# Gated cross attention with experts on one core: the second weight pair lands in the context slot, bias folds are shared by three engines, context transposes follow the query products, and 24 transposes of the identity come first

## What is computed

```python
x = x + tanh(g_xattn) * xattn(layernorm(x), ctx)
x = x + tanh(g_ffn) * ffn(layernorm(x))          # router, one of 8 experts per row

def xattn(char, sub):
    scores = (char @ Wq_c.T + bq_c) @ (sub @ Wk_s.T + bk_s).T / sqrt(512)
    char2sub = softmax(scores) @ (sub @ Wv_s.T + bv_s)
    scores2 = (sub @ Wq_s.T + bq_s) @ (char @ Wk_c.T + bk_c).T / sqrt(512)
    sub2char = softmax(scores2) @ (char @ Wv_c.T + bv_c)
    gate = sigmoid(concat(char2sub, sub2char) @ Wg.T + bg)
    return gate * char2sub + (1 - gate) * sub2char
```

## Time and profile before

| | us |
|---|---|
| median of 3 runs (lowest, highest) | 1189.27 (1188.73, 1190.29) |
| profiled execution | 1190.17 |
| its span in the profile | 1188.4 |
| TensorE busy (share of the span) | 1156.3 (97%) |
| VectorE busy | 716.0 (60%) |
| ScalarE busy | 451.1 (38%) |
| GpSimd busy | 199.2 (17%) |
| mean granted clock of TensorE over the span | 0.995 |

### The profile page before, as it was taken

How to read it: one execution, slowest core, us unless ns; L and a number is a source line. 1 busy time by engine, 2 the same in 40 slices (tenths; PEclk the granted TensorE clock), 3 DMA queues, 4 the chain that set the end, 5 groups by cost and what they waited for, 6 DMA issues and landing times.

```text
span 1188.4 us, 18063 instructions
## 1 busy us (share of the span) xinstructions
PE 1156.3 (97%) x5913; PEld 941.1 (79%) x5913; DVE 716.0 (60%) x1509; ACT 451.1 (38%) x800; POOL 199.2 (17%) x330
## 2 busy tenths in 40 slices
PE   6799999999999999999999999999999999998998
PEld 4678888888888888888888888888888887776776
DVE  6765655565457545763566466646565657787565
ACT  4333423443244324431444134423442344543342
POOL 2000000021001100110011011201020101266664
PEclk9899999999999999999999999999999999999999
DMA  6051102010201111011201020012010312586684
GB/s 231 18 169 55 45 28 98 10 48 27 79 26 39 35 62 44 21 35 62 62 21 35 26 97 20 30 33 97 9 39 0 134 45 76 196 268 186 178 238 128
DMA packets 59443, 90.63 MB, mean 76 GB/s; under 512 B 20522, under 2 KB 21062, under 8 KB 59400
## 3 DMA queue, kind: packets, MB, share of 16 engines
q1 hardware_dynamic: 49232, 64.25, 17.9%
q0 software_dynamic: 7264, 19.20, 5.0%
q10 hardware_dynamic: 2904, 6.63, 1.6%
HBM read 62.77 MB, written 29.12 MB: 77 GB/s over the span
## 4 chain that ended last, share of the span: by engine, by line
PE 92%; DVE 3%; issue 2%; another core or an unknown queue 1%; ACT 1%; POOL 0%; DMA 0%; ACTq 0%; DVEq 0%; POOLq 0%
PE mm L161 58%; PE u L980 15%; PE u L161 8%; PE tr L934 8%; PE mm L1754 1%; PE tr L161 1%; PE tr L1034 1%; DVE arena L380 0%; ACT pairs_as_f L1614 0%; DVE arena L1197 0%; DVE slot_as_f L372 0%; DMA slot_as_f<-in_L_xattn_bg 0%; DVE slot_as_f L1730 0%; ACTq L253 0%
## 5 line engine op out<-in xcount | busy, mean ns | idle before, releaser
L161 PE MATMUL mm<-arena 128*128 128x512 f32 x1536 | 375.4, 395 | 1.8 <-DVE arena L393 1.5
L161 PEld LDWEIGHTS mm<-arena 128*128 128x128 f32 x1536 | 282.7, 188 | 60.9 <-issue 2.8
L980 PE MATMUL u<-arena 128*128 128x512 f32 x768 | 189.8, 397 | 0.0
L161 PE MATMUL mm<-arena,q_pair 128*128 128x512 f32 x768 | 187.4, 399 | 0.0
L161 PEld LDWEIGHTS mm<-arena,q_pair 128*128 128x128 f32 x768 | 141.8, 188 | 31.8
L980 PEld LDWEIGHTS u<-arena 128*128 128x128 f32 x768 | 140.0, 188 | 27.4
L1197 DVE TENSOR_TENSOR arena<-tr,arena 128x512 fp32r<-128x512 f32 x144 | 96.7, 685 | 39.5 <-ACT arena L1093 17.5
L1197 DVE TENSOR_TENSOR arena<-mm,arena 128x512 fp32r<-128x512 f32 x64 | 44.2, 691 | 93.1 <-ACT arena L1084 89.9
L1080 ACT ACTIVATE q_pair<-mm,c_col 128x512 fp32r<-128x512 f32 x64 | 44.0, 688 | 132.8 <-PE mm L161 124.9
L1198 DVE SCALAR_TENSOR_TENSOR q_pair<-mm,c_col,q_pair 128x512 fp32r<-128x512 f32 x64 | 48.0, 750 | 70.2 <-ACT q_pair L1080 68.6
L161 PE MATMUL mm<-c2s_pair,arena 128*128 128x512 f32 x360 | 89.3, 397 | 0.0
(11 more groups left out here) (209 smaller groups left out, 1552.3 us busy)
## 6 DMA issues: line engine op xcount, KB each, us to landing
in_tile<-in_ctx SPq DMA_DIRECT2D x31, 256.0 KB, 2.6
x_tile<-in_x SPq DMA_DIRECT2D x29, 256.0 KB, 2.7
x_rows<-x_tile SPq DMA_DIRECT2D x29, 256.0 KB
in_tile<-in_x SPq DMA_DIRECT2D x28, 256.0 KB, 2.7
x_rows_early<-x_tile SPq DMA_DIRECT2D x28, 256.0 KB, 2.3
probs<-in_L_ffn_expert_b SPq DMA_DIRECT2D x21, 256.0 KB
slot_as_f<-in_L_ffn_expert_w SPq DMA_DIRECT2D x4, 1024.0 KB, 5.3
slot_as_f<-in_L_ffn_expert_w ACTq DMA_DIRECT2D x3, 1024.0 KB, 8.1
```

Source lines behind the costliest of these rows:

```text
L161: last = pe.matmul(bank, lhsT(a, c), rhs(b, c), start=start and n == 0, stop=stop and n == C * len(PASSES) - 1)
L980: last = pe.matmul(u_bank[m][:], v_pair[:, i % 2, a, tile(m)], pt_pair[:, i % 2, p], start=i == 0 and n == 0, stop=i == T - 1 and n == 2)
```

## The change

1. The raw second weights land in the two halves of the context slot CT instead of WV_S and WV_C. Their low parts no longer overwrite them. The first eviction of a context tile now waits for all 16 differences (`nat_lo`) and for 12 scalings.
2. The fold is split. `ACC` keeps only Wk_s times bq_c on VectorE (one instruction per chunk, a chain of four). A new step `SC` does the other three sums: ScalarE scales a chunk by its bias column into one of three buffers (12 passes in all, of which three write `folded` directly) and GpSimd adds it (nine additions of 128x512). `FOLD` becomes three steps: `FOLD0` the column of direction 0 (eight matmul records), `FOLD1` its constant and row, `FOLD2` all of direction 1. The row goes to the bank `mm0` instead of `u2`.
3. `CT0` to `CT3` move from between the queries to between the `A` steps, behind `Q03`. On TensorE `Q00` now waits for each chunk of A on its own.
4. `B` moves behind `AC02`; `AC00` no longer waits for `b_ready`. `AC02` stands ahead of the first x transposes, `XN0` behind `W02` and `XN1` to `XN3` ahead of all evictions on ScalarE. `AE` steps are mixed with `XT2`, `XT3`.
5. `WARM0`: 24 transposes of the identity on TensorE into `mm0`, which nobody reads, as soon as the identity is written.

The loads, their sizes and their order on SP are unchanged, and so is all work from `S00` on.

```diff
 def opening_steps():
-    names = """B0 W00 XS0 W01 AC00 XN0 XS1 W02 XN1 AC01 XS2 W03 XN2 XS3 XT0 XN3 XT1 AC02 ACC00 XT2 XT3 AC03
-               AE00 AE01 AE02 AE03 ACC01 ACC02 ACC03"""
+    names = """WARM0 W00 AC00 W01 XS0 AC01 W02 XS1 XN0 W03 XN1 XS2 XS3 XN2 XN3 AC02 B0 XT0 XT1 ACC00 AC03
+               AE00 AE01 XT2 XT3 AE02 AE03 ACC01 ACC02 ACC03 W10 SC00 SC01"""
...
-           [k.slot_as_f32[WV_S][:, LO], k.slot_as_f32[WV_C][:, LO]]]
+           [k.slot_as_f32[CT][:, HI], k.slot_as_f32[CT][:, LO]]]
...
+            elif kind == "SC":
+                for n in range(d + 1):
+                    if i == 0 and n == 0 and d == 0:
+                        act.wait_ge(b_ready, 1)
+                    to = folded[d][n]
+                    if i > 0:
+                        to = scaled[added[0] % SCALED]
+                        if added[0] >= SCALED:
+                            act.wait_ge(folded_up, added[0] - SCALED + 1)
+                        added[0] += 1
+                    act.activation(to, raw[d][n][:, i], ACT.Copy, scale=column(d, n, i)).then_inc(scaled_up, 1)
...
+            if kind == "SC" and c > 0:
+                for i in range(d + 1):
+                    n = added[0]
+                    if d == 0:
+                        pool.wait_ge(scaled_up, c + 1)
+                    else:
+                        pool.wait_ge(scaled_up, C + 2 * c + i + 1)
+                    if c > 1:
+                        pool.wait_ge(folded_up, n - d)
+                    pool.tensor_tensor(folded[d][i], folded[d][i], scaled[n % SCALED], ALU.add).then_inc(folded_up, 1)
+                    added[0] += 1
...
     if first:
-        names = """Q00 CT0 FOLD0 ACC10 W10 Q01 ACC11 W11 Q02 ACC12 W12 Q03 ACC13 W13 CT1 CT2 WT0 SM0 A10 XD0 XD1 WT1 A11 XD2
-                   XD3 CT3 FOLD10 AE10 AE11 WT2 A12 CD0 AE12 WT3 A13 CD1 AE13"""
+        names = """Q00 FOLD0 SC02 SC03 SC10 Q01 W11 SC11 Q02 W12 W13 Q03 WT0 FOLD1 SC12 SC13 A10 XD0 XD1 CT0 WT1 SM0 A11
+                   XD2 XD3 CT1 CT2 FOLD2 AE10 AE11 CD0 A12 AE12 WT2 CT3 CD1 A13 AE13 WT3"""
...
+                    if first and kind == "CT" and rel == 0 and i == 0:
+                        act.wait_ge(weights.nat_lo, 4 * C)
+                        act.wait_ge(weights.scaled_up, 3 * C)
```

More of the change, by code:

```diff
@@ L228, in weights_part, with column @@
     SMALL = 16 * 5
+    def column(d, n, c):
+        return b_cols[:, C * (2 * d + n) + c:C * (2 * d + n) + c + 1]
     def sync(sp):
@@ L424, in run @@
             elif kind == "FOLD":
[L425 to L426 removed]
+                if i == 0:
+                    pe.wait_ge(folded_col, C)
                     pe.wait_ge(group_lo, C)
[L428 to L431 removed]
+                else:
+                    pe.wait_ge(folded_up, (C - 1, 3 * (C - 1))[i - 1])
+                    pe.wait_ge(fold_read, i)
+                at = i // 2
+                if i != 1:
+                    for m in range(C):
+                        last = pe.matmul(bank[3][:, m:m + 1], folded[at][1][:, m * P:(m + 1) * P], ones[:, 0:1],
+                                         start=True, stop=True)
+                if i != 0:
+                    pe.matmul(bank[3][:, C:C + 1], ones, b_const[:, at:at + 1], start=True, stop=True)
+                    last = pe.matmul(row_bank[:], ones, folded[at][0], start=True, stop=True)
+                last.then_inc(fold_mm, 1)
+            elif kind == "WARM":
+                pe.wait_ge(consts, 1)
+                for n in range(WARM):
+                    pe.transpose(b_bank[:, 0:P], ident[:], ident[:])
         return run
     part = Part(sync, scalar, vector, gpsimd, tensor)
+    part.nat_lo, part.scaled_up, part.fold_read = nat_lo, scaled_up, fold_read
     part.group_mm, part.group_lo, part.router_split = group_mm, group_lo, router_split
@@ L948, in run @@
                         pe.wait_ge(xt_lo, 4 * b + 4)
-                    if i == 0 and here == 0:
-                        pe.wait_ge(weights_group_lo, C * (d + 1))
                     product(pe, bank[:], lambda a, c: arena[:, A_X + d, a, c, tile(i)],
-                            lambda p, c: arena[:, queries_of(d), p, c]).then_inc(q_mm, 1)
+                            lambda p, c: arena[:, queries_of(d), p, c], before=lambda c: (
+                                pe.wait_ge(weights_group_lo, C * d + c + 1) if i == 0 and here == 0 else None
+                            )).then_inc(q_mm, 1)
                 elif kind == "V":
@@ L960, in run @@
                         pe.wait_ge(ct_lo, 4 * b + 4)
+                        if here == 0:
+                            pe.wait_ge(weights.fold_read, 3)
                     product(pe, bank[:], lambda a, c: q_pair[:, a, c, tile(i)],
```

81 lines of the change are left out of this document (37 added, 44 removed).

## The result

| | before | after |
|---|---|---|
| median of the four runs each (lowest, highest), us | 1189.78 (1188.73, 1191.56) | 1183.10 (1182.02, 1183.87) |
| profiled execution and its span, us | 1190.17, 1188.4 | 1182.02, 1180.3 |

The ratio is 0.9942, with a 95% interval of 0.9924 to 0.9959: 0.6% faster, a small difference that the interval sets apart from none. Two more comparisons, each on its own chip time with its own runs of the kernel before, gave 0.9924 (0.9906 to 0.9942) and 0.9946 (0.9932 to 0.9959). The forecast of 1182.3 lies 0.8 from the median, inside its own range of 1181.3 to 1183.8.

A forecast was written before the change was run, and what follows sets the result against it. TensorE was taken as the bound, with only its idle or slow time in the first 67 us to win. S0 at 60.2, 7.0 sooner, gives 1189.27 - 7.0 = 1182.3 us; own range 1181.3 to 1183.8, wide range 1178.9 to 1186.3.

The forecast's parts named there:

- VectorE's four chores per chunk: Ahead of 48.80: two fold multiply-adds and two differences per chunk of second weights make TensorE's 6.16 us hole; two remain.
- Start to Q00: Opening: Q00 needs all four x tiles and starts at 24.8, 2.0 us sooner; the earlier AC00 is worth nothing by itself.
- The cold stretch: Around Q00: TensorE, nearly idle from 19.0 to 24.8, drops its clock; Q00 and the work behind it charged 1.6 us.
- Rival (a): Gap ahead of Q00: the clock stays up or TensorE's opening fills the gap, giving back 1.6: 1180.7 us; chance 0.25.
- ScalarE ahead of A10: From 31.3: three evictions, six scaling passes at 0.80 and six copies take 10.3 us before the last difference; A10 at 42.4.
- x: Ahead of FOLD2: time of one GpSimd addition of 128x512, taken as 1.2 us between bounds of 0.48 and 1.7.
- collisions: GpSimd additions beside VectorE differences, at chunks 1 to 3 and the row sums: each costs 0 to 1.2, charged 1.1 in all.
- WT5's late load: Behind S0: a doubt that work there, such as a late load of WT5, loses what was won; no size given.
- (b): GpSimd is the new bound: x at 1.7 to 2.5 puts FOLD2 2.0 to 5.2 later, 1184.3 to 1187.5 us; chance 0.15.
- (c): Scaling passes cost a plain copy and nothing collides: 1.3 + 0.8 + 1.1 less, 1179.1 us; chance 0.11.
- (d): Slower than before: VectorE's instructions hold off the additions, needing x above 3.5 us; chance 0.04 together with (e).
- (e): The change does nothing since another wait is behind the hole ahead of 48.80; chance 0.04 together with (d).

The follow-up runs named there:

- b4_small_fold: Kernel before, with VectorE's six chained multiply-adds of the second direction done on 2 of 512 columns (sums left out); 1188.21 us, ratio 0.9966.
- b_first: Changed kernel with the bias transpose B0 back in first place of the opening, ahead of W00; 1186.09 us, ratio 0.9955.
- Small_adds: Changed kernel with GpSimd's nine fold additions done on 2 of 512 columns (most fold sums left out); 1182.37 us, ratio 0.9926.
- fill_gaps: Changed kernel with 32 more idle transposes in TensorE's gaps between AC03 and Q00; 1184.48 us, ratio 0.9948.
- early_xt: Changed kernel with evictions XT0 and XT1 ahead of normalisations XN2 and XN3 on ScalarE; 1181.60 us, ratio 0.9910.

## Why the prediction was right

By its own steps, in the profiled execution of the changed kernel:

| step | forecast | measured |
|---|---|---|
| AC00 | 6.65 | 6.82 |
| XN3 ends | 19.95 | 20.64 |
| Q00 | 24.8 | 25.36 |
| clock at 0.50 | 22 to 29 | 21.7 to 28.6 |
| Q01 | 30.4 to 30.9 | 30.69 |
| hole ahead of A10; A10 | 1.8; 42.4 | 1.00; 41.65 |
| FOLD2's wait for GpSimd; FOLD2 | under 1; 50.2 | 0.23; 49.89 |
| S0 | 60.2 | 60.31 |
| S0 to S1 | 3.23 | 3.89 |

The mechanism held: VectorE's four chores per chunk set the old hole (b4_small_fold), two of them left it, and A10 waits for the differences and not for the fold. The forecast also named the fall of the clock, the waits' releasers and the size of the whole. But several terms were mis-sized and made up for each other:

- **Start to Q00.** Forecast 2.0 sooner, measured 1.4. The loads of chunk 1 landed later (its copies start at 7.75, not 7.24), and with them all that follows: XN3 ended 0.7 late, and Q00 came 4.72 behind it, where the forecast had 4.85. And the place of B0 was not worth nothing but about 0.4 (b_first).
- **The cold stretch.** Charged with 1.6, worth 0 to 1.1. The error is in the step that has FOLD0 "ready to run, because VectorE's three chained multiply-adds end at 28.7": they end at 29.7, since GpSimd's first addition holds one of them off (3.31 for 2.45). A fast Q00 only waits for them. And the charge was too high by the forecast's own terms: a fast Q00 from 24.8 would end at 27.7, FOLD0 would wait until 28.7, and 0.6 is left for the cold clock. Small_adds shows that case: the chain ends at 28.72 and FOLD0 starts at 29.41, 0.7 later, behind the cold Q00. Rival (a) took its 1.6 from the same step, and came out at nothing when fill_gaps made it true.
- **ScalarE ahead of A10.** A scaling pass was charged with 0.80 and measured 0.65, in the lower half of its bounds: with a scale column but no bias column it is nearer to the copy (0.575) than to the pass with both (0.82). For six passes that is 0.9. Together with three evictions and six copies the forecast had 10.3 from 31.3; they took 8.6, from 31.13 to 39.76, since in a full queue a copy takes 0.54 and an eviction 0.58. So ScalarE was done 1.8 sooner than forecast, and A10 only 0.75: VectorE's four last differences, with 0.73 of waiting for GpSimd in them, end at 41.60, just ahead of A10.
- **Additions.** x was 1.28 for one and 1.37 in a row, against 1.2. Their whole cost, 3.0, was under-sized: the forecast had 1.1 for collisions and 0.3 for waiting at FOLD2 (0.6 by its own prices, which bring TensorE there at 49.6 and not 49.9; its sum goes by FOLD2's start and doesn't change). The overrun of 1.6 appeared at FOLD0, A10 and WT3, as waits for VectorE.
- **WT3 and WT5.** The 0.93 ahead of WT3 was not foreseen: VectorE's queue is full there. WT5's late load was named as a doubt, with no price. Its cause is in the order of the steps: SyncE issues the load when WT3's transposes have freed the tile (issues from 60.15 on), and WT3 now stands right ahead of WT4, 4.35 ahead of WT5, where before it was 6.4 ahead (63.61 to 70.03). It was 0.39 to 0.70 in every execution with the changed order.

At S1 the changed kernel is 6.2 ahead of before, where 7.0 was forecast: terms off by up to 1.8 each left an error of 0.8, since they had both signs. The profiled runs differ by 8.15 and the medians by 6.7; the difference to 6.2 is the experts' part, which varies by more than that from execution to execution. Part of the closeness of the forecast is luck.

Of the rivals, (b) is out as put (x of 1.7 and more), but the collisions named for it are what cost most: GpSimd hardly bounds TensorE itself and takes VectorE's time. (c) had the scaling near its lower price and the collisions wrong. (d) and (e) have nothing in the traces.

The Trainium skill (TensorE: Matmul & The Clock Gate, PE-mode transpose) says that transposes don't count as activity for the clock, which made rival (a). Here 24 of them in fp32, right ahead of the first products, brought these from 628 to 389 ns, and 32 more kept the granted clock at 1.00; the measurement decides, for transposes written like these.

## What to carry to other kernels

When work is moved from VectorE to GpSimd, count each GpSimd instruction twice: once in its own queue, and once as time that it may take from VectorE's next instruction, however small that one is. Look for that cost in the waits that name VectorE. Before a cold stretch of TensorE is charged, or filled, see what the next step would wait for at full speed; if another engine is due at the same moment, the clock is worth nothing there. And when loads land differently from execution to execution, measure a change from the last event that the loads set, and not from the start: two of the readings here, of fill_gaps and of early_xt, look alike by the start of Q00 and are worth 0 and 1.7.
